# A decoder kernel: two key-partition score items issued together, and batch 1's self-attention groups placed between batch 0's cross-attention groups

## The chip, the cores and the metric

The kernel runs on one core of a Trainium2 chip. The metric is the device time of one execution in microseconds (us), lower is better. Engines: PE is TensorE (PEld its weight loads), DVE is VectorE, ACT is ScalarE, POOL is GpSimd and SP issues most transfers.

## The reference

Two decoder blocks with layer norm after each of six sub-layers, on x of 2 x 512 x 256 and a context of 2 x 1024 x 192, in float32:

```
x = layernorm(x + L0_attn(x))          # 16 heads, causal, 3 score dims and one bias dim, values of 16: "A0"
x = layernorm(x + L0_xattn(x, ctx))    # 16 heads of 16, 1024 keys: "X0"
x = layernorm(x + L0_ffn(x))           # matrices of +1 and -1
x = layernorm(x + L1_attn(x))          # 16 heads of 64: "A1"
x = layernorm(x + L1_xattn(x, ctx))    # 8 heads of 64, 1024 keys: "X1"
x = layernorm(x + L1_ffn(x))           # 8 experts, 2 picked
```

Each attention is a softmax of scores times values, then an output product. The change touches A0 and X0 alone.

## The kernel before

A0 and X0 are worked in **groups** of four heads: (layer, batch, g), 16 groups in all, in the order of the list `PAIRS`. The scores of a group are made twice. In the first pass the queries lie on the partitions, and only the row maximum is kept:

- **S1** (PE, L1576 for X0 on `x_kqF`; L1565 with the mask L1569 for A0 on `a_st`) writes the scores of two heads to one slot of `p_ring`. **M1** (DVE, L1311) reduces them to negated maxima in `halves` or `wide_max`. X0 has 16 such items a group, A0 8.
- **mt** transposes the maxima (PE L1695), and DVE adds them to the queries (`x_q`, `a_q`), so that the second pass subtracts them.

In the second pass the keys lie on the partitions, as the values product wants them:

- **S2** (PE, L1598 for X0, L1590 for A0) writes scores for 128 keys and two heads to a slot of `p_ring`. The contraction is over 32 (17) rows, so that each head uses one of four row groups of TensorE; an item has `pr` 0 or 1 and uses row groups 0, 1 or 2, 3. X0 has 16 items a group, A0 6.
- **E2** (ACT, L1135 and L1139) exponentiates the slot into `prob_a`. **CL** (DVE L1325, X0) clips it; **TM** (POOL L1047, A0) masks it.
- **PV** (PE L1621) multiplies with the values, once for two items. **DN** (ACT L1151) copies the result out, **dt** (PE L1687, DVE L1461 and L1462) and **rb** (PE L1716, DVE L1469) divide by the sums.

`p_ring` has three slots (`RING = 3`), taken in turn by S1 and S2 items as they are issued: an item waits until the one three before it has been read, an S1 item by M1, an S2 item by E2.

Everything else is a **unit**, through the single bank `p_unit`: projections q, k, v, output products **wo** (PE L1531 on `wo_rows`), transposes **xT** (L1675). After wo follow a layer norm (LS, LP, LN: DVE, POOL, DVE) and xT, and the next layer's queries need that.

`paired_stream` writes the order of all engines at build time, as a row of **passes** of one loop. A pass issues at most one S2 item (from the list `second`), at most one S1 item (from the list `first`), the CL or TM of the last one, perhaps one PV, and at most one unit. Both lists follow `PAIRS`. `may_score` lets S1 run ahead of S2 by up to two groups and four items; S2 of a group may start two passes after its mt was read. The engines run their instructions in this order and wait for one another by semaphores, so passes overlap in time.

In the program of before, passes 53 to 216 reach from the first wo of A0 to the last S2 item. Later come the feed-forward layer, A1, X1 and the experts, whose order the change does not touch.

Of the kernel before, what the change touches and what calls it, by code (L numbers as in the profile page):

```python
# [100 lines left out]
PAIRS = [(L, b, g) for L in ("A0", "X0") for b in range(B) for g in range(4)]  # L101
# [43 lines left out]
def paired_stream(sched, chains):  # L145
# [8 lines left out]
    pending, owed, clean, adds, keep = [], [], [], [], []  # L154
# [17 lines left out]
    while f < len(first) or s < len(second) or pending or owed or clean or adds or keep or any(heads):  # L172
# [188 lines left out]
def build_schedule():  # L361
    sched = Schedule()

    def used(n):

        return [("S2", prob_items(PAIRS[n])[-1])] if n >= 0 else []

    def a0_start(b):
# [4 lines left out]
        for g in range(4):  # L373
            out.append(step("DS", "A0", b, g, after=[UD("q", "A0", b)] + used(4 * b + g - HELD)))
# [5 lines left out]
    def x0_keys(b, g):  # L380
        n = 4 * b + g - HELD
        return [unit("k", "X0", b, g, h, after=used(8 + n) if n >= 0 else []) for h in range(2)]

    def x0_queries(b, g):
        n = 4 * b + g - HELD
        return [unit("q", "X0", b, g, after=[turned_x("A0", b)] + (used(8 + n) if n >= 0 else []))]
# [116 lines left out]
def decoder(nc, d, out):  # L503
# [29 lines left out]
    with ctx:  # L533
# [240 lines left out]

        def pair_back(grp, k):
# [78 lines left out]
        def _(sp):  # L854
# [75 lines left out]
            for kind, key in sched.steps:  # L930
# [11 lines left out]
                if L == "A0":  # L942
# [7 lines left out]
                    if grp >= HELD:  # L950
                        wait(sp, "S2", *prob_items(PAIRS[grp - HELD])[-1])
# [46 lines left out]
        def _(pool):  # L998
# [31 lines left out]
            for kind, key in sched.steps:  # L1030
                if kind == "KF":
# [4 lines left out]
                    if 4 * b + g >= HELD:  # L1036
                        wait(pool, "S1", *max_items(PAIRS[8 + 4 * b + g - HELD])[-1])
# [53 lines left out]
        def _(act):  # L1091
# [14 lines left out]
            for kind, key in sched.steps:  # L1106
# [60 lines left out]
                elif kind == "UA":  # L1167
# [18 lines left out]
                    elif u[0] in ("q", "k") and u[1] == "X0":  # L1186
                        _, L, b, g = u[:4]
                        place, part = (4 * b + g) % HELD, u[4] if u[0] == "k" else 2
                        if 4 * b + g >= HELD:
                            wait(act, "S2", *prob_items(PAIRS[8 + 4 * b + g - HELD])[-1])  # L1190
# [41 lines left out]
        def _(dve):  # L1232
# [41 lines left out]
            for kind, key in sched.steps:  # L1274
# [250 lines left out]
        def _(pe):  # L1525
# [8 lines left out]
            for kind, key in sched.steps:  # L1534
# [20 lines left out]
                elif kind == "S1":  # L1555
# [4 lines left out]
                    if L == "A0":  # L1560
                        pe.wait_ge(a0_stacked[G % HELD], 16 * 8 * (G // HELD + 1))
                        w = 128 * (i + 1)
                        for aa in range(2):
                            r = 64 * pr + 32 * aa
                            nc.tensor.matmul(o[:, aa, 0:w], a0_st[r:r + 17, G % HELD, 1, 128 * i:128 * i + 128],  # L1565
                                             a0_st[r:r + 17, G % HELD, 0, 0:w], start=True, stop=False,
# [310 lines left out]
```

## Time and profile before

| | before |
|---|---|
| median of 3 runs | 1334.27 us (1333.01 to 1334.39) |
| the profiled execution | 1329.35 us, its span 1327.6 us |
| PE, DVE, ACT busy, share of the span | 90%, 56%, 42% |
| TensorE's clock as granted, mean over the span | 0.956 |

A profile row gives the start, the duration, the engine, the line, the operation, and what is written and read. A busy share is time in which some instruction of the engine is under way; matmuls are pipelined, so a busy PE may still have room. A float32 matmul of the program is two records in the trace (S2, PV and the units; `x4` for the two heads of one S2 item), an S1 matmul is one. Granted clock 1.00 is TensorE's 2.4 GHz level, 0.50 its 1.2 GHz level. An idle time in brackets names what ended it.

### The profile page before, as it was taken

To read this page: it belongs to the slowest core of one execution; us is meant where nothing else is said; L and a number is where in the kernel's file an instruction comes from. 1 tells how busy PE (TensorE), PEld (TensorE's weight loads), DVE (VectorE), ACT (ScalarE), POOL (GpSimd) and SP (SyncE) were. 2 spreads that over 40 slices of the span, in tenths; PEclk is the share of its full clock that TensorE was granted. 3 is DMA by queue.
4 is the path that set the end of the run, shared out by engine and by line. 5 is a ranking of instruction groups with operands and counts; after the bars stand their busy time and mean duration, and the time that the engine had idled before them with its cause. 6 is when DMAs were issued, how large, how long until landed. Compare 5 with 4: busy or idle time off the path is not lost.

```text
span 1327.6 us, 20645 instructions
## 1 busy us (share of the span) xinstructions
PE 1193.6 (90%) x7754; PEld 754.9 (57%) x7754; DVE 742.4 (56%) x1099; ACT 556.9 (42%) x1070; POOL 89.6 (7%) x127
## 2 busy tenths in 40 slices
PE   5999887899999986889599999999999999998887
PEld 3454444233332234778367777767777777777545
DVE  3346476888898845453256554655455554554322
ACT  1343332555555641221156663655334444453230
POOL 1112211000000003000000000000000000000120
PEclk9898877999999987999799999999999999999989
DMA  5010002000000002000242331223443333120000
GB/s 169 9 49 18 8 1 64 0 1 1 1 1 1 1 1 80 0 0 1 68 119 65 80 80 33 65 64 81 113 120 80 80 81 81 31 50 1 0 16 16
DMA packets 46917, 57.47 MB, mean 43 GB/s; under 512 B 12635, under 2 KB 25446, under 8 KB 46822
## 3 DMA queue, kind: packets, MB, share of 16 engines
q1 hardware_dynamic: 43062, 52.48, 16.3%
q10 hardware_dynamic: 3760, 3.67, 0.9%
q8 instruction: 66, 1.08, 0.3%
q14 instruction: 29, 0.24, 0.1%
HBM read 15.23 MB, written 3.15 MB: 14 GB/s over the span
## 4 chain that ended last, share of the span: by engine, by line
PE 79%; DVE 9%; issue 6%; ACT 3%; POOL 1%; DMA 1%; SPq 1%; POOLq 0%; ACTq 0%; DVEq 0%
PE p_unit L1531 21%; PE p_ring L1531 11%; PE p_ring L1632 9%; PE p_out L1655 8%; PE p_ring L1551 8%; PE p_ring L1598 7%; PE p_out L1621 6%; PE p_unit L1716 2%; PE p_ring L1576 2%; PE p_unit L1675 1%; DVE probT_b L1341 1%; PE p_ring L1590 1%; DVE stats L1244 1%; POOL m_z L1064 1%; PE p_ring L1569 1%
## 5 line engine op out<-in xcount | busy, mean ns | idle before, releaser
L1153 ACT ACTIVATE probT_b<-p_ring 128x512 f32<-128x512 f32 x144 | 84.5, 598 | 260.4 <-PE p_ring L1632 260.0
L1311 DVE TENSOR_REDUCE halves<-p_ring 128x2 f32<-128x1024 f32 x128 | 155.6, 1218 | 40.9 <-PE p_ring L1576 40.7
L1341 DVE COPY probT_b<-p_ring 128x512 f32<-128x512 f32 x112 | 77.4, 691 | 174.0 <-PE p_ring L1632 174.0
L1135 ACT ACTIVATE prob_a<-p_ring 128x1024 f32<-128x1024 f32 x128 | 130.7, 1023 | 93.8 <-PE p_ring L1598 93.8
L1293 DVE TENSOR_REDUCE nmax<-p_ring 128x2 f32<-128x1024 f32 (+1 forms) x128 | 155.9, 1218 | 23.5 <-PE p_ring L1551 23.5
L1121 ACT ACTIVATE prob_b<-p_ring,nmax 128x512 f32<-128x512 f32 (+1 forms) x192 | 158.7, 835 | 2.6 <-DVE nmax L1293 2.3
L1551 PE MATMUL p_ring<-stacks 128*128 128x512 f32 x512 | 150.8, 417 | 4.5 <-ACT prob_b L1121 4.5
L1632 PE MATMUL p_ring<-ident,prob_b 128*128 128x128 f32 x1024 | 134.6, 274 | 0.0
L1632 PEld LDWEIGHTS p_ring<-ident,prob_b 128*128 128x128 f32 x1024 | 115.8, 141 | 27.7 <-issue 25.8
L1598 PE MATMUL p_ring<-x_q,x_kq 32*128 32x512 f32 x512 | 126.5, 656 | 0.0
L1551 PEld LDWEIGHTS p_ring<-stacks 128*128 128x128 f32 x512 | 87.0, 190 | 17.0 <-ACT prob_b L1121 5.1
L1325 DVE TENSOR_SCALAR prob_a<-prob_a 128x1024 f32<-128x1024 f32 x128 | 89.5, 700 | 8.6 <-ACT prob_a L1135 8.6
L1311 DVE TENSOR_REDUCE wide_max<-p_ring 128x2 f32<-128x256 f32 (+3 forms) x64 | 52.5, 823 | 66.4 <-PE p_ring L1569 66.3
L1576 PE MATMUL p_ring<-x_kqF 32*128 32x512 f32 x256 | 66.6, 518 | 16.8 <-ACT prob_a L1135 15.9
L1598 PEld LDWEIGHTS p_ring<-x_q,x_kq 32*128 32x128 f32 x512 | 38.3, 188 | 68.7 <-issue 48.5
L1621 PE MATMUL p_out<-prob_a,x_v 128*32 128x512 f32 x512 | 69.9, 618 | 2.7 <-issue 1.8
L1655 PE MATMUL p_out<-probT_b,a_v 128*64 128x128 f32 x1024 | 70.0, 279 | 0.0
L1655 PE MATMUL p_out<-probT_b,x_v 128*64 128x128 f32 x1024 | 69.6, 279 | 0.0
L1655 PEld LDWEIGHTS p_out<-probT_b,a_v 128*64 128x64 f32 x1024 | 54.6, 136 | 23.4 <-issue 17.5
L1655 PEld LDWEIGHTS p_out<-probT_b,x_v 128*64 128x64 f32 x1024 | 54.6, 136 | 21.9 <-issue 11.3
L1531 PE MATMUL p_unit<-ctxT,x_wk 128*128 128x512 f32 x128 | 66.1, 641 | 0.4
L1487 DVE TENSOR_TENSOR splitL_b<-p_unit,splitH_b 128x512 fp32r<-128x512 f32 x44 | 30.4, 691 | 60.3 <-ACT splitH_b L1198 54.2
(201 smaller groups left out, 1658.6 us busy)
## 6 DMA issues: line engine op xcount, KB each, us to landing
stacks<-splitH_b SPq DMA_DIRECT2D x144, 128.0 KB, 2.4
stacks<-splitL_b SPq DMA_DIRECT2D x144, 128.0 KB, 2.4
a_st<-a_image SPq DMA_DIRECT2D x64, 32.0 KB, 1.8
ctx_raw<-in_ctx ACTq DMA_DIRECT2D x1, 1536.0 KB, 15.5
x<-in_x ACTq DMA_DIRECT2D x2, 512.0 KB, 5.2
k_words<-in_L_ffn_k SPq DMA_DIRECT2D x1, 1024.0 KB, 6.7
a_wq<-in_L_attn_Wq SPq DMA_DIRECT2D x1, 1024.0 KB, 6.2
a_wo<-in_L_attn_Wpost SPq DMA_DIRECT2D x1, 1024.0 KB, 9.3
```

What stands on the lines that cost most here:

```text
L1121: ins = nc.scalar.activation(prob_b[:, n % NP_SLOTS, a * 512:a * 512 + w_all], p_scores[:, n % 2, a * 512:a * 512 + w_all], ACT.Exp, bias= ...
L1135: nc.scalar.activation(prob_place(key), slot_of("S2", key), ACT.Exp, accum_out=x0_sums[:, m:m + 1]).then_inc(done["E2"], 1)
L1293: nc.vector.tensor_reduce(nmax[:, n % 4, 0:heads], src, AX.X, ALU.max, negate=True).then_inc(done["M"], 1)
L1311: nc.vector.tensor_reduce(to, src, AX.X, ALU.max, negate=True).then_inc(done["M1"], 1)
L1341: keep_turned(dve, key, lambda o, i: nc.vector.tensor_copy(o, i)).then_inc(done["VD"], 1)
L1531: ins = nc.tensor.matmul(o, a, m, start=(n == 0), stop=(n == len(pairs) - 1))
L1551: ins = nc.tensor.matmul(p_scores[:, n % 2, 512 * a:512 * a + 512], st[:, q_at:q_at + 128], st[:, k_at:k_at + 512], start=(part == 0), sto ...
L1576: ins = nc.tensor.matmul(o[:, aa, :], x0_kqF[r:r + 32, place, 2, 128 * i:128 * i + 128], x0_kqF[r:r + 32, place, hf, :], start=True, stop= ...
L1598: ins = nc.tensor.matmul(o[:, aa, :], x0_kq[r:r + 32, place, j // 4, 128 * (j % 4):128 * (j % 4) + 128], x0_q2[r:r + 32, G % 2, :], start= ...
L1621: ins = nc.tensor.matmul(p_out[32 * a:32 * a + 32, lo:T], v, prob_place((*key, a // 2))[:, a % 2, at:at + T - lo], start=(c == 0), stop=end)
L1632: ins = nc.tensor.transpose(p_turn[:, half, 128 * j:128 * j + 128], prob_b[:, n % NP_SLOTS, 128 * bl:128 * bl + 128], ident[:, :])
L1655: ins = nc.tensor.matmul(p_out[rows * a:rows * a + rows, 128 * i:128 * i + 128], values(L, b, h, j), probT[:, n % places, 4 * in_tile + j ...
```

## The change

Two edits. First, `PAIRS` no longer finishes A0 of batch 1 before X0 of batch 0: after A0 (1,0) and (1,1) come X0 (0,0), A0 (1,2), X0 (0,1), A0 (1,3), and then the other X0 groups. Second, S2 items are issued two at a time, `pr` 0 and 1, every second pass, so that four heads on four row groups stand together; their E2s still go one to a pass. The rest adapts the addressing: places in `a0_st`, `x0_kq` and `x0_kqF` come from batch and g in place of the position in `PAIRS`, and waits name the group by layer.

```diff
-PAIRS = [(L, b, g) for L in ("A0", "X0") for b in range(B) for g in range(4)]
+PAIRS = ([("A0", 0, g) for g in range(4)] + [("A0", 1, 0), ("A0", 1, 1), ("X0", 0, 0), ("A0", 1, 2), ("X0", 0, 1)]
+         + [("A0", 1, 3), ("X0", 0, 2), ("X0", 0, 3)] + [("X0", 1, g) for g in range(4)])
...
         fresh = []
-        if s < len(second) and age("UD", "mt", *second[s][:3]) >= 2:
-            it = second[s]
-            s += 1
-            sched.add("S2", *it)
+        if not scored and s < len(second) and age("UD", "mt", *second[s][:3]) >= 2:
+            for it in second[s:s + 2]:
+                sched.add("S2", *it)
+                scored.append(it)
+            s += 2
+        if scored:
+            it = scored.pop(0)
             sched.add("E2", *it)
             fresh.append(it)
...
+        def place_of_heads(grp):
+
+            return (4 * grp[1] + grp[2]) % HELD
...
                     else:
-                        place = (G - 8) % HELD
+                        place = place_of_heads((L, b, g))
```

On PE, in the middle of an X0 group with no unit near, the program of before has this (L1598 is S2, L1576 is S1, L1621 is PV):

```order
L1598 MATMUL p_ring<-x_q,x_kq 128x512 x2
L1576 MATMUL p_ring<-x_kqF 128x512 x2
L1598 MATMUL p_ring<-x_q,x_kq 128x512 x2
L1576 MATMUL p_ring<-x_kqF 128x512 x2
L1621 MATMUL p_out<-prob_a,x_v 32x512 x4
```

The changed program has this, where the lines have moved by 13 (L1611 is S2, L1589 S1, L1634 PV):

```order
L1611 MATMUL p_ring<-x_q,x_kq 128x512 x4
L1589 MATMUL p_ring<-x_kqF 128x512 x2
L1634 MATMUL p_out<-prob_a,x_v 32x512 x4
L1589 MATMUL p_ring<-x_kqF 128x512 x2
```

Two S2 items of two heads have become one run of four heads, the first S1 item stands behind all four, and the second S1 item behind PV.

On PE, where S1 of X0 (0,0) is issued, the program of before has this (L1590 is S2 of A0, L1687 and L1716 are dt and rb):

```order
L1590 MATMUL p_ring<-a_q,a_st 128x512 x2
L1576 MATMUL p_ring<-x_kqF 128x512 x2
L1590 MATMUL p_ring<-a_q,a_st 128x384 x2
L1576 MATMUL p_ring<-x_kqF 128x512 x2
L1687 MATMUL p_unit<-ident,raw 128x128 x4
L1590 MATMUL p_ring<-a_q,a_st 128x384 x2
L1576 MATMUL p_ring<-x_kqF 128x512 x2
```

The changed program has this there, up to the first v unit of batch 1's X0 (L1544 on `x_wv`):

```order
L1589 MATMUL p_ring<-x_kqF 128x512 x4
L1700 MATMUL p_unit<-ident,raw 128x128 x4
L1589 MATMUL p_ring<-x_kqF 128x512 x2
L1729 MATMUL p_unit<-ident,rwide_a 128x128 x4
L1589 MATMUL p_ring<-x_kqF 128x512 x24
L1544 MATMUL p_unit<-x_wv,ctxT 128x256 x4
```

No S2 item is left between the S1 items: fifteen of the sixteen stand in these rows, with dt and rb alone between them.

On PE, the two wo units of A0 batch 1 stand like this in the program of before:

```order
L1531 MATMUL p_unit<-wo_rows,outT_a 128x256 x8
L1576 MATMUL p_ring<-x_kqF 128x512 x2
L1695 MATMUL p_unit<-ident,wide_max 128x128 x4
L1576 MATMUL p_ring<-x_kqF 128x512 x2
L1531 MATMUL p_unit<-wo_rows,outT_a 128x256 x8
```

In the changed program they come much later, in X0 (0,2):

```order
L1611 MATMUL p_ring<-x_q,x_kq 128x512 x4
L1589 MATMUL p_ring<-x_kqF 128x512 x2
L1544 MATMUL p_unit<-wo_rows,outT_a 128x256 x8
L1589 MATMUL p_ring<-x_kqF 128x512 x2
L1544 MATMUL p_unit<-wo_rows,outT_a 128x256 x8
L1611 MATMUL p_ring<-x_q,x_kq 128x512 x4
```

Before, only S1 work stood around them; now S2 work does too.

## Rows read from the trace of the kernel before

**Rows 1.** The page: busy time by engine; granted clock in 40 slices.

```profile
PE 1193.6 (90%) x7754; PEld 754.9 (57%) x7754; DVE 742.4 (56%) x1099; ACT 556.9 (42%) x1070; POOL 89.6 (7%) x127
...
PEclk9898877999999987999799999999999999999989
```

**Rows 2.** The page: shares of the chain that ended last.

```profile
PE 79%; DVE 9%; issue 6%; ACT 3%; POOL 1%; DMA 1%; SPq 1%; POOLq 0%; ACTq 0%; DVEq 0%
```

**Rows 3.** Windows: length, then busy time (and instructions) of PE, PEld, DVE, ACT, POOL; clock.

```profile
124.00:215.00 91.00, 79.35 (x460) 44.18 (x460) 52.82 (x80) 24.00 (x33) 16.02 (x29) 0.85 0.03 7
...
324.00:456.00 132.00, 122.79 (x697) 39.72 (x696) 116.31 (x147) 74.03 (x136) 5.55 (x9) 1.00 0.00 1
```

**Rows 4.** Timeline of DVE in X0, no unit near.

```profile
341.57 1.21 DVE L1311 TENSOR_REDUCE halves<-p_ring 128x2 f32<-128x1024 f32 x1
342.70 0.68 DVE L1325 TENSOR_SCALAR prob_a<-prob_a 128x1024 f32<-128x1024 f32 x1
343.30 1.22 DVE L1311 TENSOR_REDUCE halves<-p_ring 128x2 f32<-128x1024 f32 x1
...
350.52 1.22 DVE L1311 TENSOR_REDUCE halves<-p_ring 128x2 f32<-128x1024 f32 x1 [0.21 <-PE p_ring L1576]
```

**Rows 5.** Timeline of PE and ACT in the same stretch.

```profile
345.53 0.70 PE L1598 MATMUL p_ring<-x_q,x_kq 32*128 32x512 f32 x2
345.55 0.50 PE L1576 MATMUL p_ring<-x_kqF 32*128 32x512 f32 x2
...
346.71 1.02 ACT L1135 ACTIVATE prob_a<-p_ring 128x1024 f32<-128x1024 f32 x1 [1.58 <-PE p_ring L1598]
...
347.88 0.50 PE L1576 MATMUL p_ring<-x_kqF 32*128 32x512 f32 x2 [0.45 <-ACT prob_a L1135]
348.31 1.07 PE L1621 MATMUL p_out<-prob_a,x_v 128*32 128x512 f32 x8
```

**Rows 6.** Timeline of PE in X0 where units k and q stand.

```profile
326.51 1.98 PE L1531 MATMUL p_unit<-ctxT,x_wk 128*128 128x512 f32 x4
328.42 0.70 PE L1598 MATMUL p_ring<-x_q,x_kq 32*128 32x512 f32 x2
...
329.48 1.98 PE L1531 MATMUL p_unit<-xT,x_wq 128*128 128x512 f32 x4
```

**Rows 7.** Timeline of PE after the last S1 item.

```profile
471.13 1.14 PE L1598 MATMUL p_ring<-x_q,x_kq 32*128 32x512 f32 x8
472.20 1.06 PE L1621 MATMUL p_out<-prob_a,x_v 128*32 128x512 f32 x8
473.20 1.13 PE L1598 MATMUL p_ring<-x_q,x_kq 32*128 32x512 f32 x6
```

**Rows 8.** Timeline of DVE (S1 without CL) and of ACT (S2 without S1).

```profile
171.12 3.47 DVE L1311 TENSOR_REDUCE halves<-p_ring 128x2 f32<-128x1024 f32 x3
...
473.32 1.02 ACT L1135 ACTIVATE prob_a<-p_ring 128x1024 f32<-128x1024 f32 x1
...
474.38 1.02 ACT L1135 ACTIVATE prob_a<-p_ring 128x1024 f32<-128x1024 f32 x1
```

**Rows 9.** Timeline of ACT in A0.

```profile
118.59 1.02 ACT L1139 ACTIVATE prob_a<-p_ring 128x1024 f32<-128x1024 f32 x1 [3.46 <-PE p_ring L1590]
...
124.71 0.81 ACT L1139 ACTIVATE prob_a<-p_ring 128x768 f32<-128x768 f32 x1 [1.17 <-PE p_ring L1590]
```

**Rows 10.** Timeline of PE: units v, wo and xT of batch 1.

```profile
184.80 3.78 PE L1531 MATMUL p_unit<-x_wv,ctxT 128*128 128x256 f32 x8
...
189.99 1.99 PE L1531 MATMUL p_unit<-x_wv,ctxT 128*128 128x256 f32 x8
...
198.85 5.38 PE L1531 MATMUL p_unit<-wo_rows,outT_a 128*128 128x256 f32 x16 [0.67 <-DVE outT_a L1469]
...
207.52 3.72 PE L1531 MATMUL p_unit<-wo_rows,outT_a 128*128 128x256 f32 x16 [0.63 <-DVE x_q L1455]
```

**Rows 11.** Window at the low clock, columns as in rows 3.

```profile
219.80:233.50 13.70, 11.91 (x44) 4.33 (x44) 8.84 (x11) 4.76 (x9) 2.35 (x1) 0.50 0.06 11
```

More of the change, by code:

```diff
@@ L153, in paired_stream @@
     heads = [list(c) for c in chains]
-    pending, owed, clean, adds, keep = [], [], [], [], []
+    pending, owed, clean, adds, keep, scored = [], [], [], [], [], []
     f = s = n = 0
@@ L170, in ready @@
         return item[0] <= n and all(a in sched.at for a in item[2])
-    while f < len(first) or s < len(second) or pending or owed or clean or adds or keep or any(heads):
+    while f < len(first) or s < len(second) or pending or owed or clean or adds or keep or scored or any(heads):
         while pending:
@@ L373, in a0_start @@
         for g in range(4):
-            out.append(step("DS", "A0", b, g, after=[UD("q", "A0", b)] + used(4 * b + g - HELD)))
+            out.append(step("DS", "A0", b, g, after=[UD("q", "A0", b)] + used("A0", 4 * b + g - HELD)))
         return out
@@ L381, in x0_keys @@
         n = 4 * b + g - HELD
-        return [unit("k", "X0", b, g, h, after=used(8 + n) if n >= 0 else []) for h in range(2)]
+        return [unit("k", "X0", b, g, h, after=used("X0", n)) for h in range(2)]
     def x0_queries(b, g):
         n = 4 * b + g - HELD
-        return [unit("q", "X0", b, g, after=[turned_x("A0", b)] + (used(8 + n) if n >= 0 else []))]
+        return [unit("q", "X0", b, g, after=[turned_x("A0", b)] + used("X0", n))]
     last_one = prob_items(PAIRS[-1])[-1]
@@ L950, in _ @@
                     if grp >= HELD:
-                        wait(sp, "S2", *prob_items(PAIRS[grp - HELD])[-1])
+                        wait(sp, "S2", *prob_items(("A0", (grp - HELD) // 4, (grp - HELD) % 4))[-1])
                     for which in range(2):
@@ L1036, in _ @@
                     if 4 * b + g >= HELD:
-                        wait(pool, "S1", *max_items(PAIRS[8 + 4 * b + g - HELD])[-1])
+                        wait(pool, "S1", *max_items(x0_back(b, g))[-1])
                     nc.gpsimd.tensor_copy(x0_kqF[:, place, part, :], x0_kq[:, place, part, :]).then_inc(done["KF"], 1)
@@ L1189, in _ @@
                         if 4 * b + g >= HELD:
-                            wait(act, "S2", *prob_items(PAIRS[8 + 4 * b + g - HELD])[-1])
+                            wait(act, "S2", *prob_items(x0_back(b, g))[-1])
                         if u[0] == "q":
@@ L1564, in _ @@
                             r = 64 * pr + 32 * aa
-                            nc.tensor.matmul(o[:, aa, 0:w], a0_st[r:r + 17, G % HELD, 1, 128 * i:128 * i + 128],
-                                             a0_st[r:r + 17, G % HELD, 0, 0:w], start=True, stop=False,
+                            nc.tensor.matmul(o[:, aa, 0:w], a0_st[r:r + 17, place_of_heads(key[:3]), 1, 128 * i:128 * i + 128],
+                                             a0_st[r:r + 17, place_of_heads(key[:3]), 0, 0:w], start=True, stop=False,
                                              tile_position=(r, 0))
@@ L1594, in _ @@
                     else:
-                        place = (G - 8) % HELD
+                        place = place_of_heads((L, b, g))
                         for aa in range(2):
```

15 lines of the change are left out of this document (9 added, 6 removed).

## The prediction

> **What bounds the kernel now.** I read the page first. PE is busy 90% of the span and DVE 56% [rows 1], and the chain that ended last lies on PE for 79% [rows 2]. So a change to the order counts where it lets PE wait less or do less. The clock slices [rows 1] show 8, 8, 7, 7 in slices 4 to 7 (33.2 us each, so 100 to 232 us), which hold the end of A0 and the start of X0, and 9 in the seven slices behind them.
>
> Then I read the windows. From the first wo of A0 to the first S2 of X0 (124 to 215 us) PE is busy for 79.35 of 91 us at clock 0.85, and DVE for 52.82, so DVE stands idle for 38 us [rows 3]. In the X0 groups of batch 1 (324 to 456 us) PE is busy for 122.79 of 132 us, and DVE for 116.31, 88% [rows 3]. Here two engines are near their limits together.
>
> The timeline says which of them sets the pace. With no unit near, M1 follows CL by 0.60 us and CL follows M1 by 1.13 us, so DVE alone wants 1.73 us a pass. From 341.57 to 350.52 us lie five passes, 1.79 us each [rows 4]. DVE sets this pace. PE there runs S2 and S1 at once: S1 starts 0.02 us after S2, on other row groups [rows 5]. Where units stand, PE sets the pace: unit k takes 1.91 us up to the next S2, and S2 with its S1 hidden beneath takes 1.06 us up to the next unit [rows 6].
>
> **Edit one, four heads back to back.** I cost two passes of X0 on PE.
> - Before: two S2 with hidden S1 (2 x 1.06) [rows 6] and one PV (1.00, from 472.20 to 473.20 us) [rows 7] make 3.12 us.
> - After: four heads together take 1.07 us (eight records, from 471.13 to 472.20 us; four records took 1.06) [rows 6]. But all four row groups are now taken, so the first S1 stands behind S2, and the second, behind PV, has no S2 beside it either. Each costs 0.43 us (from 347.88 to 348.31 us) [rows 5]. With PV that is 2.93 us.
>
> So a pair saves 0.19 us of PE, not 1.06. It saves nothing at all where DVE sets the pace. There another loop comes near. S2, S2, S1, S1 share three slots, so the first S1 of a pair of passes takes the slot of the S1 just before it. It must wait for that M1 to end: M1 1.22, a release, S1 0.50 [rows 5]. With 0.07 us for two releases that is 1.79 us from M1 to M1 against 1.73, so two passes take 3.52 to 3.6 us, as now. ACT's loop is shorter: E2 starts 1.18 us after S2 (345.53 to 346.71) [rows 5], two E2 take 2 x 1.06 [rows 8], 3.3 us in all. For A0 I see the same exchange with smaller pieces. About a dozen pairs lie beside k and q in X0, which saves 2 us; the dt and rb units lose about as much, because their PE work now queues behind an S1 that is out in the open. I take 0 for this edit, with -9 (some 45 full pairs at 0.19) and +8 (the same 45, were the two releases 0.18 us slower together) as bounds.
>
> The Trainium skill has a rule that speaks for the edit: the page TensorE: Matmul & The Clock Gate, section Part 3: Packing small matmuls, gives four row tiles of 512 columns a speedup of 3.07 over running them one by one. Rows 7 agree that four heads cost what two cost. By that rule alone the sum would lose one S2 for every pair.
>
> **Edit two, A0 and X0 alternate.** It removes and adds no work; it changes which items meet in a pass. I counted the passes of the two programs by what they issue, S1 / S2, from the first wo of A0 to the last S2: 164 before, 185 now. S1 of X0 (0,0) now stands alone (the second place of the order shown above), and the lead that `may_score` allows is counted in groups, so that an A0 group of 6 items holds back an X0 group of 16. The prices are from the rows, with bounds where no row has the case.
> - X0 / X0: 109 to 89, at 1.79 [rows 4]: -35.8.
> - A0 / A0: 13 to 1, at 1.53 (118.59 to 124.71 us, four passes) [rows 9]: -18.4.
> - X0 / none: 12 to 27, at 1.16 (3.47 us for three) [rows 8]: +17.4.
> - none / X0: 19 to 29, at 1.06 (473.32 to 474.38 us) [rows 8]: +10.6.
> - A0 / none: 4 to 6, at 1.53: +3.1.
> - X0 / A0: 7 to 12. Before, at DVE's 1.16. Now the pair's loop of M1, release and S1 has no CL to hide in: half of (1.79 + 1.16), 1.48. 12 x 1.48 - 7 x 1.16: +9.6. (At 1.16 it would be +5.8.)
> - A0 / X0: 0 to 10. No row shows it. The bounds are ACT's 1.06 and the X0 pace of 1.79; I take half of ACT's loop of 3.3, 1.65: +16.5 (+10.6 to +17.9).
> - none / A0: 0 to 7. Bounds 0.81 (E2 alone) [rows 9] and 1.53; I take 1.1: +7.7.
> - none / none: 0 to 4, units alone: 0, as they are counted below.
>
> The sum is +10.7 us. One list alone is cheap for a pass, but 1.16 and 1.06 make 2.22 us for what one full pass does in 1.79.
>
> **The units that move.** The order of edit two puts batch 1's two wo beside S2 work, and the four v beside S1 of A0. PE still needs 3.72 us for each wo and 1.99 for each v [rows 10], and the ring gives DVE and ACT at most three slots to live on meanwhile, so they are not hidden. What can be gained is clock: the first v took 3.78 and the first wo 5.38 us [rows 10], 1.79 and 1.66 us more than their fellows. I take -3 for that and for a layer norm with more work beside it. The bounds are 0, if the new stretch of S1 alone (PE at work 0.43 of 1.16 us) takes the clock down ahead of the v units again, and -15, over a third of DVE's 38 idle us [rows 3] refilled. Transfers play no part: the a_st loads wait for A0's S2 items, which come no later than their use needs, and later stages load early.
>
> **Sum.** 0 + 10.7 - 3, so +8 us. The profiled execution took 1329.35 us, 1.75 of it outside its span of 1327.6; with the change it would take 1337.4. The median of the runs lies 4.9 us above the profiled execution, so I predict 1342 us. A difference within 0.2% (2.7 us) could hardly be told from none.
>
> **Rivals.**
> - *The alternation fills the idle time* (faster). DVE's 38 idle us from 124 to 215 us [rows 3] and A0's light items under X0's S2 are what speaks for it: the refill is then -15, the two unseen kinds of pass cost their lower bounds (-6 -4 -2 against the sum), and the pairs save 7 of the 9 us: 10.7 - 12 - 15 - 7, about -23 at the very best; with half of each, 10.7 - 6 - 10 - 5, -10: 1324 us. It decides when refill and pairs together pay over 11 us. Against it: 21 more passes. Chance 0.22.
> - *The pairs pay in full* (faster), as by the rule of the page above. 64 pairs at 1.06 us are 68 us of PE, but DVE's busy share of 88% in X0 [rows 3] leaves 12% of the 260 us or so from 215 us on, 31 us, and the alternation takes 8 back: 1311 us. Against it: S1 is hidden now. Chance 0.03.
> - *The clock falls* (slower still). In two full passes PE would have 2.93 us of work in 3.55 us, against 3.12 in 3.58 now, and the new stretches of S1 alone have 0.43 us in 1.16 [rows 5, 8]. At 0.50 DVE was busy for 8.84 of 13.7 us, 65% against 88% [rows 11, 3], so a stretch there costs a quarter of its length. With 40 us more at 0.50: +10, 1352 us. For it: slices 6 and 7 stand at 7 already, behind passes of this thin kind at 171 us [rows 1, 8]. Against: it held in slices 8 to 14, where full passes ran. Chance 0.18.
> - *Nothing to measure*: the singles cost less and the refill pays for them. 1334 us. Chance 0.12.
>
> The Trainium skill's page TensorE: Matmul & The Clock Gate, section Why this matters for your kernels, warns of PE idle gaps between bursts; by that the third rival would be likelier than I put it, and [rows 1] agree in that the dips lie where PE is least busy.
>
> **Numbers.** The forecast itself (1335 to 1349) has 0.45. Slower by over 0.2%: 0.45 and 0.18, 0.63. Same: 0.12. Faster: 0.22 and 0.03, 0.25. The range goes from 1322, which takes in half-successful filling, to 1355 for the clock.
>
> **What would show it.** In the profile after: eight S2 records in 1.14 us with S1 after them; full X0 passes still at 1.75 to 1.8 us; S1 of X0 (0,0) as sixteen reductions 1.16 us apart with ACT idle for 25 us or more; the first S2 of X0 (0,3) 5 to 12 us later than now; the last X0 group ending about 8 us later; the rest of the span unchanged. I am wrong on edit one if an X0 group of batch 1 takes over 1 us less or over 2 us more than now, and on edit two if S2 of X0 (0,3) starts earlier than now. What would make the forecast fail most easily is the clock, which my prices hold at 1.00.

## The result, and the profile after

| | before | after |
|---|---|---|
| median | 1333.64 us (1327.12 to 1334.39, 4 runs) | 1364.03 us (1360.38 to 1368.97, 4 runs) |
| ratio | | 1.0243, 95% interval 1.0204 to 1.0282 |
| span of the profiled execution | 1327.6 us | 1362.2 us |
| mean granted clock | 0.956 | 0.927 |

The change costs 30 us. The forecast of 1342 us had the direction, and its range ended at 1355, 9 us below the median. The ratios below leave out two executions of other kernels, one of run 5 (1695.4 us at a clock of 0.64, and its trace is of this one) and one of run 13 (1355.4 us).

The kernel before stood beside the runs in 58 more executions, at mean clocks of 0.938 to 0.954 and 1327.0 to 1342.4 us. Its profiled one had 0.956, more than any of them, so what is read below from one trace against another holds somewhat more clock than the medians do.

The page of the changed kernel: busy times, granted clock in slices of 34.1 us, and the shares of the chain that ended last.

```profile
PE 1204.9 (88%) x7754; PEld 762.5 (56%) x7754; DVE 744.4 (55%) x1099; ACT 552.3 (41%) x1070; POOL 90.0 (7%) x127
...
PEclk7996778687999998799899999999999999999998
...
PE 72%; DVE 17%; issue 5%; ACT 3%; DMA 1%; POOL 1%; SPq 1%; POOLq 0%; DVEq 0%; ACTq 0%
```

Against [rows 1, 2], PE's busy time is only 11 us longer, and the chain has moved from PE (79% to 72%) to DVE (9% to 17%). The clock slices 4 to 10 (102 to 341 us) read 6, 7, 7, 8, 6, 8, 7, where slices 4 to 10 of before read 8, 8, 7, 7, 9, 9, 9.

Where the end of the interleaving stands is shown by the first E2 of X0 (0,3), the first E2 of X0 (1,0) and the last E2 of X0. Timeline of ACT after:

```profile
363.72 1.02 ACT L1148 ACTIVATE prob_a<-p_ring 128x1024 f32<-128x1024 f32 x1 [0.47 <-PE p_ring L1611]
...
399.62 1.02 ACT L1148 ACTIVATE prob_a<-p_ring 128x1024 f32<-128x1024 f32 x1 [0.47 <-PE p_ring L1611]
...
516.97 1.02 ACT L1148 ACTIVATE prob_a<-p_ring 128x1024 f32<-128x1024 f32 x1
```

These three stood at 325.63, 360.98 and 481.10 us before. So the changed kernel is 38.1 us late at X0 (0,3), 38.6 at X0 (1,0), and 35.9 at the end of X0. The whole loss is made by 364 us.

Windows of the kernel before (length, then busy time of PE, PEld, DVE, ACT, POOL, granted clock): up to the first E2 of X0 (0,3), from pass 53 on, passes 37 to 53, and from pass 53 to the first reduction of X0.

```profile
0.00:325.70 325.70, 281.40 (x1640) 131.49 (x1644) 202.88 (x291) 127.39 (x210) 43.73 (x87) 0.92 0.12 33
125.20:325.70 200.50, 177.52 (x1048) 76.91 (x1048) 144.88 (x195) 82.69 (x141) 23.15 (x36) 0.90 0.05 13
100.90:125.20 24.30, 22.45 (x188) 11.13 (x184) 16.64 (x26) 11.40 (x15) 5.83 (x12) 0.84 0.10 24
125.20:169.40 44.20, 38.75 (x250) 20.21 (x246) 22.24 (x40) 14.67 (x21) 11.80 (x19) 0.90 0.03 7
```

The same windows of the changed kernel, and last its stretch of X0 (0,0) reductions alone:

```profile
0.00:364.00 364.00, 304.55 (x1648) 140.85 (x1652) 203.99 (x291) 125.63 (x211) 45.45 (x88) 0.81 0.10 29
131.50:364.00 232.50, 196.89 (x1052) 84.91 (x1052) 145.50 (x195) 81.40 (x141) 24.70 (x37) 0.79 0.04 11
102.00:131.50 29.50, 27.16 (x188) 13.15 (x190) 16.82 (x25) 11.03 (x15) 5.84 (x13) 0.67 0.07 19
131.50:169.40 37.90, 29.92 (x134) 15.14 (x134) 8.07 (x19) 9.03 (x13) 9.13 (x13) 0.76 0.03 7
169.40:187.90 18.50, 12.80 (x57) 5.92 (x58) 18.41 (x18) 0.87 (x2) 0.62 (x1) 0.62 0.00 1
```

A window's clock of c means that 2 x (1 - c) of its length ran at 0.50 (1.2 GHz) and the rest at 1.00 (2.4 GHz). From pass 53 to X0 (0,3) the kernel before has 40 us at 0.50 in 200.5, the changed one 98 in 232.5. Passes 37 to 53 hold the same work in both, but for the pairs: 24.3 us at 0.84 and 29.5 at 0.67 (they come back in run 8). And in the window up to the first reduction of X0, which stands at 169.4 us in both kernels, DVE worked 22.24 us before and 8.07 after.

### The profile page after: what moved, and what is told of

The parts are those of the page before. It is cut to its first block, busy times and chain, and to the rows that moved or that the text cites. A ratio compares the mean times of both kernels' runs of the same rounds, so it can differ in the third digit from the quotient of the medians.

```text
span 1362.2 us, 20645 instructions
## 1 busy us (share of the span) xinstructions
PE 1204.9 (88%) x7754; PEld 762.5 (56%) x7754; DVE 744.4 (55%) x1099; ACT 552.3 (41%) x1070; POOL 90.0 (7%) x127
## 4 chain that ended last, share of the span: by engine, by line
PE 72%; DVE 17%; issue 5%; ACT 3%; DMA 1%; POOL 1%; SPq 1%; POOLq 0%; DVEq 0%; ACTq 0%
PE p_unit L1544 20%; PE p_ring L1544 11%; PE p_ring L1645 8%; PE p_out L1668 8%; PE p_ring L1564 7%; DVE halves L1324 6%; PE p_out L1634 4%; PE p_ring L1611 4%; DVE prob_a L1338 2%; PE p_unit L1729 2%; PE p_unit L1688 1%; PE p_ring L1578 1%; PE p_ring L1589 1%; DVE probT_b L1354 1%; DVE stats L1257 1%
## 5 line engine op out<-in xcount | busy, mean ns | idle before, releaser
L1611 PE MATMUL p_ring<-x_q,x_kq 32*128 32x512 f32 x512 | 85.4, 689 | 12.2 <-ACT prob_a L1148 12.0
L1589 PE MATMUL p_ring<-x_kqF 32*128 32x512 f32 x256 | 73.5, 596 | 11.2 <-DVE halves L1324 10.0
L1589 PEld LDWEIGHTS p_ring<-x_kqF 32*128 32x128 f32 x256 | 25.4, 204 | 87.9 <-DVE halves L1324 40.9
L1634 PE MATMUL p_out<-prob_a,x_v 128*32 128x512 f32 x512 | 71.6, 632 | 0.5 <-issue 0.5
L1544 PE MATMUL p_unit<-ctxT,x_wk 128*128 128x512 f32 x128 | 65.3, 633 | 1.5 <-ACT x_kq L1208 1.3
```

The lines of the kernel that those rows point to most:

```text
L1544: ins = nc.tensor.matmul(o, a, m, start=(n == 0), stop=(n == len(pairs) - 1))
L1589: ins = nc.tensor.matmul(o[:, aa, :], x0_kqF[r:r + 32, place, 2, 128 * i:128 * i + 128], x0_kqF[r:r + 32, place, hf, :], start=True, stop= ...
L1611: ins = nc.tensor.matmul(o[:, aa, :], x0_kq[r:r + 32, place, j // 4, 128 * (j % 4):128 * (j % 4) + 128], x0_q2[r:r + 32, G % 2, :], start= ...
L1634: ins = nc.tensor.matmul(p_out[32 * a:32 * a + 32, lo:T], v, prob_place((*key, a // 2))[:, a % 2, at:at + T - lo], start=(c == 0), stop=end)
```

## The experiments

All times are beside runs of the kernel before on the same chip, whose medians were 1334.3 to 1335.8 us. In short:

| kernel | median, us | ratio, 95% interval |
|---|---|---|
| pairs alone (1) | 1352.49 | 1.0143 (1.0094 to 1.0192) |
| order alone (2) | 1358.44 | 1.0177 (1.0137 to 1.0218) |
| after, S1 three times (3) | 1377.31 | 1.0333 (1.0277 to 1.0390) |
| before, S1 three times (4) | 1338.82 | 1.0038 (1.0011 to 1.0065) |
| old order, pairs of X0 (5) | 1334.24 | 0.9995 (0.9968 to 1.0021) |
| old order, pairs of A0 (6) | 1352.15 | 1.0131 (1.0080 to 1.0182) |
| new order, pairs of X0 (7) | 1352.08 | 1.0127 (1.0061 to 1.0192) |
| order alone, S1 twice (8) | 1365.85 | 1.0220 (1.0175 to 1.0265) |
| weakened order, no pairs (9) | 1341.93 | 1.0050 (1.0031 to 1.0069) |
| as 6, S1 ahead of the pair (10) | 1347.80 | 1.0118 (1.0066 to 1.0169) |
| as 9, pairs of X0 (11) | 1338.39 | 1.0021 (0.9998 to 1.0043) |
| old order, pairs of A0 batch 1 (12) | 1343.37 | 1.0071 (1.0040 to 1.0103) |
| old order, pairs of A0 batch 0 (13) | 1348.35 | 1.0085 (1.0049 to 1.0120) |

**1. The pairs alone.**

```diff
-PAIRS = ([("A0", 0, g) for g in range(4)] + [("A0", 1, 0), ("A0", 1, 1), ("X0", 0, 0), ("A0", 1, 2), ("X0", 0, 1)]
-         + [("A0", 1, 3), ("X0", 0, 2), ("X0", 0, 3)] + [("X0", 1, g) for g in range(4)])
+PAIRS = [(L, b, g) for L in ("A0", "X0") for b in range(B) for g in range(4)]
```

> The changed kernel with the old order of head groups: edit one (two passes' S2 matmuls issued together) alone. Theory A (the time is mostly TensorE's clock: the trace of the changed kernel has 170.6 us at a granted clock of 0.50 before its time 600, against 88.6 before the change): the pairs leave the order alone, so 1334 to 1342, with low-clock time as in the kernel before. Theory B (more passes and passes that hold one kind of work cost it): 1334, since the number of passes is unchanged. Theory C (the pairs cost it, by the 6 us that the all-A0 stage to step 53 lost and 0.5 us in each of the eight X0 groups): 1342 to 1346. My own forecast had edit one at 0.

It measured +18, more than any theory gave. An edit that I had put at 0 costs over half of the loss by itself. Its trace puts nearly all of it ahead of X0's second passes: pass 78, which lies behind A0's last reduction (pass 69), is 28.8 us late in that execution, the first E2 of X0 (0,3) 31 us, and the last E2 of X0 28 us.

**2. The order alone.**

```diff
-            for it in second[s:s + 2]:
-                sched.add("S2", *it)
-                scored.append(it)
-            s += 2
+            it = second[s]
+            s += 1
+            sched.add("S2", *it)
```

> The changed kernel with one S2 issued per pass, as before: edit two (the order of head groups) alone. Theory A (clock): 1352 to 1362, with some 50 us or more of added time at a granted clock of 0.50 in the stretch from 125 to 360. Theory B (the ledger of passes, which my forecast priced at +10.7 less 3): 1342, with the clock as before. Theory C (pairs): what the whole change cost less what the pairs alone do, 1355.

It measured +24, inside theory A's range of times. The two parts sum to 42 us and the whole is 30, so they overlap. Windows of it, as above: up to the first E2 of X0 (0,3), from pass 53, passes 37 to 53.

```profile
0.00:351.00 351.00, 296.56 (x1640) 137.19 (x1644) 202.87 (x291) 127.19 (x210) 43.66 (x87) 0.84 0.11 30
127.60:351.00 223.40, 191.81 (x1048) 82.67 (x1048) 144.45 (x195) 82.86 (x141) 23.18 (x36) 0.83 0.04 11
98.60:127.60 29.00, 27.90 (x188) 13.40 (x192) 16.87 (x25) 11.38 (x15) 5.80 (x12) 0.62 0.07 20
```

The first window is 25.3 us longer than before, with the same number of PE instructions (1640), and has 112 us at 0.50 against 52. But in the order that `paired_stream` writes, this kernel and the one before are the same up to pass 53. So the second window is what the order can account for: 22.9 us longer, with 76 us at 0.50 against 40. These 36 us are fewer than the 50 that theory A wanted, and the other 24 of the 60 us at 0.50 fell into passes that the order does not touch.

**3 and 4. Keeping TensorE busy**, in the changed kernel and in the one before.

```diff
+    beside = {sched.when[(kind, key)] for kind, key in sched.steps if kind == "E2" and key[0] == "X0"}
+
+    def times(key):
+        return 1 if sched.when[("S1", key)] in beside else 3
...
+                        for again in range(times(key)):
                             for aa in range(2):
```

> The changed kernel with every S1 matmul of X0 done three times over, with the same result, in the passes that have no E2 of X0 (the passes in which VectorE's reduction sets the pace and TensorE streams for less than half of it). Nothing is left out, six matmul instructions stand where two stood. Theory A: TensorE is busier where it idled, the 0.50 stretches between 150 and 335 shrink by half or more, and 10 to 20 us of the 30 come back, to 1344 to 1354. Theories B and C: the repeats are work added to passes that VectorE bounds, so nothing comes back, 1364, or up to 10 us more where they run at half clock and become the bound.

> The kernel before with the same repeats of S1 of X0 in passes without an E2 of X0. Theory A: the 20 us or so at 0.50 between 175 and 234 of the kernel before shrink, and with them 3 to 8 us, 1326 to 1331. Theories B and C: no gain, 1334 to 1340.

Nothing came back: 13 us more than the changed kernel, and 4 more than the one before. Three S1 at 0.43 us would want 1.29 us in a pass of 1.13, but in the stretch of X0 (0,0) reductions the repeats were no bound: twelve reductions took 13.66 us, as in the changed kernel (13.67). Windows of that stretch in the kernel of 3:

```profile
174.76:179.30 4.54, 3.53 (x24) 1.63 (x20) 4.54 (x6) 0.00 (x0) 0.00 (x0) 1.00 0.01 4
179.30:188.40 9.10, 8.97 (x40) 6.45 (x41) 9.10 (x9) 0.00 (x0) 0.00 (x0) 0.50 0.00 0
```

The clock fell to 0.50 in the middle of the repeats and stayed there while PE was busy for 8.97 of 9.10 us. So more work for PE did not hold it up here. Where the 13 us are lost stays open; the profiled execution loses 9 of them by X0 (0,3), behind that stretch. Run 8 repeats less.

**5 and 6. Which pairs cost.** Both keep the old order.

```diff
-            for it in second[s:s + 2]:
+            together = 2 if second[s][0] == "X0" else 1
+            for it in second[s:s + together]:
                 sched.add("S2", *it)
                 scored.append(it)
-            s += 2
+            s += together
```

(and "A0" for "X0" in the other)

> Old order, S2 issued in pairs for X0's items only, singly for A0's. In the trace of the pairs-alone kernel the E2 of A0's step 53 comes 14.6 us later than before and the groups of X0 stand at the distances of before. Theory D: a pair takes two of the three score slots, so that the S1 of its pass waits for VectorE's reduction of the pass before, and that costs only in A0, where the reductions set the pace; TensorE sets it in X0. Then this kernel is at 1331 to 1338, no change. Theory C, all pairs cost by their count (24 of A0's to 64 of X0's): 1346 or so.

> Old order, pairs for A0's items only. Theory D: the whole +18 of the pairs-alone kernel, 1348 to 1356, with a part of it (8 or so) in stretches where the S1 of a pair's pass waits at the full clock, and the rest in time at a granted clock of 0.50 between 98 and 160. Theory C: 1339.

64 of 88 pairs are X0's and cost nothing; the 24 of A0 cost all 18 us. Theory D foretold these times. It says that a pair takes two of the three slots, so that an S1 waits for the reduction of the pass before. In passes of A0 without a unit such waits can be read. The kernel before, PE and then DVE:

```profile
95.60 0.44 PE L1565 MATMUL p_ring<-a_st 17*128 17x384 f32 x2
...
96.19 0.44 PE L1590 MATMUL p_ring<-a_q,a_st 17*128 17x384 f32 x2
96.99 0.44 PE L1565 MATMUL p_ring<-a_st 17*128 17x384 f32 x2 [0.36 <-ACT prob_a L1139]
```

```profile
96.30 0.96 DVE L1311 TENSOR_REDUCE wide_max<-p_ring 128x2 f32<-128x768 f32 x1 [0.92 <-PE p_ring L1569]
97.68 0.96 DVE L1311 TENSOR_REDUCE wide_max<-p_ring 128x2 f32<-128x768 f32 x1 [0.42 <-PE p_ring L1569]
```

And the kernel with pairs of A0, passes 34 and 35, PE and then DVE:

```profile
95.19 0.44 PE L1578 MATMUL p_ring<-a_st 17*128 17x384 f32 x2
...
96.11 0.55 PE L1603 MATMUL p_ring<-a_q,a_st 17*128 17x384 f32 x4 [0.26 <-ACT prob_a L1152]
96.90 0.44 PE L1578 MATMUL p_ring<-a_st 17*128 17x384 f32 x2 [0.24 <-DVE wide_max L1324]
```

```profile
95.89 0.96 DVE L1324 TENSOR_REDUCE wide_max<-p_ring 128x2 f32<-128x768 f32 x1 [0.80 <-PE p_ring L1582]
97.60 0.96 DVE L1324 TENSOR_REDUCE wide_max<-p_ring 128x2 f32<-128x768 f32 x1 [0.75 <-PE p_ring L1582]
```

With pairs, S1 at 96.90 us waits for DVE: its slot is that of the reduction at 95.89, which has only just ended at 96.85. The next reduction starts at 97.60, and DVE stood idle 0.75 us, where it stood 0.42 in the kernel before. There the S1 at 96.99 waits for ACT, and the reduction of the pass before (96.30) is still running, so they overlap.

Passes 25 to 33, one A0 group with its units, are at a clock of 1.00 in both, and show what a group pays. Windows of the kernel before (with passes 17 to 78, and 78 to X0 (0,3), for what follows):

```profile
54.70:182.30 127.60, 116.16 (x794) 60.41 (x792) 70.95 (x104) 53.29 (x73) 29.09 (x55) 0.89 0.07 20
182.30:325.70 143.40, 127.27 (x723) 51.34 (x724) 111.43 (x144) 62.35 (x114) 8.44 (x11) 0.92 0.05 15
75.20:94.70 19.50, 18.86 (x132) 11.75 (x128) 7.90 (x13) 8.53 (x14) 2.91 (x6) 1.00 0.15 43
```

and of the kernel with pairs of A0:

```profile
54.40:206.70 152.30, 138.56 (x796) 69.16 (x800) 72.26 (x105) 53.12 (x73) 29.82 (x56) 0.72 0.06 17
206.70:345.40 138.70, 122.34 (x720) 48.76 (x721) 111.25 (x144) 61.58 (x113) 7.77 (x10) 0.95 0.06 16
73.90:94.40 20.50, 19.48 (x136) 11.99 (x132) 8.10 (x13) 8.55 (x14) 3.06 (x6) 1.00 0.14 41
```

19.5 us become 20.5, so the pairs cost 1.0 us a group at the full clock; for eight groups that is 8 us, an estimate. But this isn't the wait of theory D. PE is busy for 19.48 of 20.5 us there and DVE for 8.10, so PE sets the pace, and none of PE's idle time there ends with an S1 or S2 that waited for a slot. What has changed is what PE hides. The kernel before, where units stand:

```profile
77.47 0.50 PE L1590 MATMUL p_ring<-a_q,a_st 17*128 17x512 f32 x2
77.48 0.44 PE L1565 MATMUL p_ring<-a_st 17*128 17x384 f32 x2
...
78.23 1.99 PE L1531 MATMUL p_unit<-x_wv,ctxT 128*128 128x256 f32 x8
```

and the kernel with pairs of A0:

```profile
78.98 0.45 PE L1603 MATMUL p_ring<-a_q,a_st 17*128 17x384 f32 x4
79.27 0.34 PE L1578 MATMUL p_ring<-a_st 17*128 17x384 f32 x2
...
82.15 0.46 PE L1603 MATMUL p_ring<-a_q,a_st 17*128 17x256 f32 x8
82.64 0.50 PE L1578 MATMUL p_ring<-a_st 17*128 17x512 f32 x2
```

Before, S2 starts 0.01 us ahead of S1 and lies wholly beneath S1 and its mask, which take 0.76 us up to the unit. With pairs, S1 starts 0.29 and 0.49 us behind the first of the two S2, and 0.34 us in the third pair of the group (93.52 to 93.86 us): 1.12 us in all. The passes that now have no S2 save nothing, for S1 and mask alone still take 0.75 us up to the unit (76.31 to 77.06 us). That is about the 1.0 us measured.

From pass 17 to 78 the loss is 24.7 us in this execution, and the clock of that stretch fell from 0.89 to 0.72, 57 us more at 0.50. Behind pass 78, where the two programs are the same, it is 4.7 us faster than before, at 0.95 against 0.92.

**7. The new order with pairs of X0 only.** The diff is the first of 5, on the changed kernel.

> The new order with pairs for X0's items only, A0's singly. Theory D: the changed kernel less what the pairs of A0 cost it, which the two parts' sum (+18 and +24 against +30 for both) puts at 6: 1356 to 1360, as the order alone. If pairs of X0 cost something in the interleaved stretch, where A0's S1 stands beside X0's S2: 1360 to 1364.

1352.08: below both expectations. A0's pairs are worth 12 us of the changed kernel, and X0's pairs beside A0's reductions seem to save some 6 against the order alone, but the intervals overlap, and the four executions are two of 1346 us at clocks of 0.939 and 0.941 and two of 1358 and 1360 us at 0.929. So this can be the clock of two executions.

**8. The order alone, S1 doubled in passes without any E2.** As 3, with `beside` over the E2 of both layers and 2 for 3.

> The new order with S2 issued singly, and every S1 matmul of X0 done twice in the passes that have no E2 of any kind (some 29 passes, in which a reduction of 1.13 us sets the pace and S1 takes 0.43 us at the full clock, so that 0.86 still hides). Nothing is left out. Theory A (the rest of the order's +24 over the ledger's +8 is time at 0.50): the low-clock time between 164 and 191 shrinks and the units and passes right behind it run at the full clock, 1348 to 1355. Theory B: 1358, no change, since those passes wait for the reductions at either clock; up to 1362 if two matmuls at half clock (1.7 us) outlast the reduction.

Theory A's cure fails: 1365.85, and the clock is no higher. Windows of this kernel: passes 37 to 53, and the 16 reductions of X0 (0,0) alone.

```profile
99.60:131.40 31.80, 31.44 (x188) 14.36 (x192) 16.95 (x24) 11.31 (x15) 5.83 (x12) 0.50 0.08 18
166.00:185.30 19.30, 16.96 (x86) 8.53 (x84) 18.44 (x19) 0.60 (x1) 0.62 (x1) 0.62 0.00 1
```

In the second, PE was busy for 16.96 of 19.3 us, against 12.99 of 18.7 in the order alone, and the clock is 0.62 in both. The first lies ahead of every doubled instruction, and holds the same work as in the order alone, but took 31.8 us at 0.50 against 29.0 at 0.62. More kernels give it with the same work: 24.3 us at 0.84 before, and the new order with pairs of X0, and last run 11 below:

```profile
99.00:124.90 25.90, 24.57 (x189) 11.88 (x192) 16.64 (x25) 11.42 (x15) 5.82 (x12) 0.76 0.09 22
...
100.20:132.05 31.85, 31.49 (x188) 14.42 (x192) 16.98 (x25) 11.36 (x15) 5.80 (x12) 0.50 0.07 18
```

These lie on a line: 24.3, 25.9, 29.0 and 31.8 us with 7.8, 12.4, 22.0 and 31.8 us at 0.50, which is (31.8 - 24.3) / (31.8 - 7.8) = 0.31 us lost for each us at 0.50. Run 4 (25.2 us at 0.76) and run 9 (28.7 at 0.62) lie near it.

In the order that `paired_stream` writes, all seven kernels are the same up to pass 53. So what differs between these seven is not the change of order. The two with the old order have the least time at 0.50, but it is one execution of each, and they can't say whether that is more than chance. The clock has a price there; what sets it stays open.

**9 to 11. A weaker order, and the ring or the queue.**

```diff
-PAIRS = ([("A0", 0, g) for g in range(4)] + [("A0", 1, 0), ("A0", 1, 1), ("X0", 0, 0), ("A0", 1, 2), ("X0", 0, 1)]
-         + [("A0", 1, 3), ("X0", 0, 2), ("X0", 0, 3)] + [("X0", 1, g) for g in range(4)])
+PAIRS = ([("A0", 0, g) for g in range(4)] + [("A0", 1, 0), ("A0", 1, 1), ("A0", 1, 2), ("X0", 0, 0)]
+         + [("A0", 1, 3), ("X0", 0, 1), ("X0", 0, 2), ("X0", 0, 3)] + [("X0", 1, g) for g in range(4)])
```

> S2 issued singly, and the new order weakened: the key order is A0 of batch 0 (4 groups), A0 of batch 1 groups 0 to 2, X0(0,0), A0(1,3), X0(0,1) and the rest. The passes that hold an S1 or an E2 are 219 up to pass 249, against 211 before and 230 in the order alone. Theory B (the number of passes prices it; the order alone has 19 more and costs 24): 8/19 of 24, 1344. Theory E (the order's cost is that S1 of X0(0,0), which must wait for batch 0's layer norm, stands ahead of A0(1,2)'s S1, so that no reduction runs for about 31 us and 16 of X0 then run alone): A0(1,2)'s S1 fill that time again as they do before, and little is left, 1334 to 1338. Theory A (clock): anywhere between, with 0.2 to 0.34 us for each us more at a granted clock of 0.50 than before's 55 up to the first E2 of X0(0,3).

> The weakened order of the one-crossing kernel with pairs for X0's items only. Pairs of X0 were worth nothing in the old order and 6 us (1352 against 1358, intervals touching) in the new one. If those 6 us are real and come from passes in which X0's S2 stands beside A0's reductions: 3 us below the one-crossing kernel. If they were chance of the clock: the same as it within 3.

+7 us, where the count of passes gives +10 and theory E up to +4. It lies between the two and tells neither out. Most of the order's cost is gone when A0 (1,2) may be reduced while batch 0's layer norm runs; the passes are fewer too, so this doesn't show which of the two did it. With pairs of X0 the median is another 3.5 us lower, as expected if run 7's 6 us were real, but the intervals overlap.

Run 10, in the loop that writes the schedule:

```diff
+        begin = not scored and s < len(second) and age("UD", "mt", *second[s][:3]) >= 2
+        early = begin and second[s][0] == "A0"
+        if early:
+            reduce_one()
...
+        if not early:
+            reduce_one()
```

(`reduce_one` is the block that adds S1 and M1.)

> Old order, pairs for A0's items only, and in a pass that begins a pair the S1 and its reduction ahead of the two S2 instead of behind them. Theory D1 (the score ring: with three slots, two taken by a pair, every S1 of one of the two passes takes the slot of the reduction just before it, and cannot overlap it): the slots come round in the same cycle, nothing is gained, 1348 to 1356. Theory D2 (TensorE's queue: the S1 stands behind two S2 that wait for ScalarE): the S1 is free of them and 8 or more us come back, 1334 to 1344.

1347.80 is at the lower edge of D1's 1348 to 1356 and 4 us outside D2's. Passes 25 to 33 take 20.8 us in its trace, against 20.5 with S1 behind the pair and 19.5 without pairs. So in that stretch nothing is gained, and an S1 that stands behind waiting S2 isn't what costs. This doesn't speak for the ring alone: with S1 first, the pair stands in the open behind the mask (from 94.56 to 95.00 us in its trace), where it would cost as much. No run kept the pairs and gave the ring a fourth slot, so the two aren't told apart by a run; the rows above are what speaks for the work in the open.

**12 and 13. Half of the pairs of A0.**

```diff
-            together = 2 if second[s][0] == "A0" else 1
+            together = 2 if second[s][:2] == ("A0", 1) else 1
```

(and 0 for 1 in the other)

> Old order, pairs only for the A0 items of batch 1 (four of the eight A0 groups); those of batch 0, before step 48, go singly. Theory D with the ring's price alone, 1.0 us a group (passes 25 to 33, at the full clock in both kernels, take 20.5 us with pairs and 19.5 without): 1338. If the clock's share belongs to the pairs too, half of the 18: 1343. If it is chance that fell in passes 37 to 53, which hold singles here: 1338 to 1340.

> Old order, pairs only for the A0 items of batch 0. Ring alone: 1338. With the clock's share bound to the pairs of passes 37 to 48 (wholly at 0.50 in both traces with pairs in them and old order): 1343 to 1348, and then the two halves' surpluses over before should sum to the 17 to 18 of all A0 pairs.

By their ratios they cost 9.5 and 11.4 us, 21 in all, against 17.5 for both halves at once. Each costs more than the 4 us of four groups at 1.0 (both intervals lie above it), so the rest comes with the pairs too. The traces, one execution of each, have it at the pairs: with pairs in batch 1 only, passes 37 to 53 take 24.5 us as before and passes 53 to 64 take 38.7 against 31.8; with pairs in batch 0 only, it is 32.6 and 33.9. That alone would be weak, since run 11 has 31.8 us in passes 37 to 53 without a pair of A0.

## Why the prediction fell short

**Edit one, put at 0 (bounds -9 and +8), measured +18.** This is the step that failed, and in it the sentence on A0. For X0 the working held. The changed kernel in X0, PE and then DVE:

```profile
381.80 1.07 PE L1634 MATMUL p_out<-prob_a,x_v 128*32 128x512 f32 x8
382.80 0.50 PE L1589 MATMUL p_ring<-x_kqF 32*128 32x512 f32 x2
383.52 1.24 PE L1611 MATMUL p_ring<-x_q,x_kq 32*128 32x512 f32 x8 [0.22 <-ACT prob_a L1148]
384.93 0.50 PE L1589 MATMUL p_ring<-x_kqF 32*128 32x512 f32 x2 [0.17 <-DVE halves L1324]
```

```profile
381.92 1.22 DVE L1324 TENSOR_REDUCE halves<-p_ring 128x2 f32<-128x1024 f32 x1
...
383.65 1.22 DVE L1324 TENSOR_REDUCE halves<-p_ring 128x2 f32<-128x1024 f32 x1
...
385.47 1.23 DVE L1324 TENSOR_REDUCE halves<-p_ring 128x2 f32<-128x1024 f32 x1
```

The eight records of S2 take 1.24 us (I said 1.14, and 1.07 in the sum), S1 starts 1.41 us after them, it waits for the M1 before it (the loop that I described, "M1 1.22, a release, S1 0.50"), and two passes take 3.55 us (381.92 to 385.47), in the forecast 3.52 to 3.6. Pairs of X0 alone measured 0.9995. What failed is the one sentence on A0, "the same exchange with smaller pieces". It is not the same exchange. In X0 an S2 with its S1 beneath takes 1.06 us and S1 alone 0.43, so a pair takes two long pieces together and puts two short ones in the open. In A0 the longer piece is S1 with its mask, 0.76 us, and S2 was hidden beneath it; a pair puts S2's 0.29 to 0.49 us in the open and saves nothing. Where no unit stands, the waits for the ring come on top (0.26 us for ACT and 0.24 for DVE in passes 34 and 35). X0 has a CL of 0.6 us behind each M1, under which the next S1 is written; in A0 DVE has nothing between two M1. Together that is 1.0 us a group at the full clock where it was measured. My bound of +8 was worked out for X0's pairs, and that it equals eight groups of A0 is luck. The other 10 us I had no term for: they go with time at 0.50, 57 us more from pass 17 to 78. At 0.31 those would be 18, and 18 + 8 overstates the 24.7 us there by little.

**Edit two, put at +10.7 for the ledger and -3 for units, measured +24.** From pass 53 on, where the order begins to differ, the order alone is 22.9 us longer up to X0 (0,3), with 36 us more at 0.50. At 0.31 that is 11 us and leaves 12, more than the forecast's 7.7 and near the ledger's 10.7 without the gain that I took for the units. This is an estimate: the price is from passes 37 to 53 alone, a clock is given to 0.01, which is up to 2 us of each window at 0.50, and where reductions set the pace the price is nothing, as the next rows show, which would leave more for the ledger. So the ledger's sum is not refuted, and not confirmed to better than a few us. What it lacked is what the forecast said of it, the clock, "which my prices hold at 1.00". The weaker order (8 more passes for +7, where 19 cost 24) costs less for each pass, but within the intervals.

**The units.** I gave -3 for a better clock of v and wo. The pair of wo of batch 1 in the changed kernel:

```profile
314.87 4.90 PE L1544 MATMUL p_unit<-wo_rows,outT_a 128*128 128x256 f32 x16
...
321.34 3.72 PE L1544 MATMUL p_unit<-wo_rows,outT_a 128*128 128x256 f32 x16 [1.15 <-DVE stats L1257]
```

4.90 and 3.72 us against 5.38 and 3.72 [rows 10]: 0.5 us gained. Against it stands what I did not cost, and what no run here prices by itself. `first` is a queue. S1 of X0 (0,0) must wait for the layer norm of batch 0, as it did before, and now stands ahead of the S1 of A0 (1,2). Timeline of DVE and then of ACT after:

```profile
169.42 3.57 DVE L1324 TENSOR_REDUCE halves<-p_ring 128x2 f32<-128x1024 f32 x3 [13.48 <-PE p_ring L1589]
...
175.46 13.67 DVE L1324 TENSOR_REDUCE halves<-p_ring 128x2 f32<-128x1024 f32 x12
```

```profile
190.33 0.60 ACT L1224 ACTIVATE x_v<-p_unit 128x512 f32<-128x512 f32 x1 [19.50 <-PE p_unit L1544]
...
198.20 1.02 ACT L1148 ACTIVATE prob_a<-p_ring 128x1024 f32<-128x1024 f32 x1 [0.47 <-PE p_ring L1611]
```

The reductions of X0 start at 169.42 us after 13.48 idle us, no earlier than before (169.38), and A0's 16 reductions that used to be done by then are still to come. So the shape that I foretold is there, sixteen reductions 1.13 us apart (I said 1.16). ACT is then idle for 19.50 us in one piece (I said 25 or more), and the stretch is at a clock of 0.62 without loss: the last twelve reductions, at 0.50 throughout, come as fast as those of [rows 8].

**The rivals.** "The clock falls" (0.18) happened, and larger: I allowed 40 us more at 0.50 for +10, and there were 86 us more up to X0 (0,3) (138 against 52). Its price of a quarter is near the 0.31 measured. What it had as the reason, PE with less to do, isn't shown: in run 8 passes 37 to 53 stood at 0.50 with PE busy for 31.44 of 31.80 us. That the clock "held in slices 8 to 14, where full passes ran" stayed true behind 364 us only. The alternation didn't fill idle time: DVE stood idle for more of 131 to 169 us than before. In its price is a slip: half of 15 and of 7 are 7.5 and 3.5, not 10 and 5, so its middle case should have read -6 and 1328 us. "Pairs pay in full" (0.03) was rightly small.

**How much is the clock.** The 58 executions of the kernel before give a price with not an instruction changed. A straight line through their times and their time at 0.50 (from the mean clocks) has 0.29 us for each us at 0.50, 95% interval 0.23 to 0.35. By the mean clocks of all their executions, the pairs alone, the order alone and the pairs of A0 spend 40 to 42 us more at 0.50 than the kernel before beside them, the two halves of A0's pairs 17 and 23, and the changed kernel about 52. At 0.29 that is 12 us for each of the first three, 5 and 7 for the halves, and 15 of the changed kernel's 30. Of the mean times it leaves some 6 us for the pairs of A0 (8 by the count of groups), 4 for each half (4 by the same count), and 13 for the order. These are estimates.

**What stays open** is why the clock falls more with A0's pairs and with the new order. That it does is shown by the mean clocks: 0.926 to 0.931 in the four executions of the changed kernel, 0.931 to 0.934 in those of the order alone, 0.929 to 0.932 with pairs of A0, and 0.938 to 0.954 in the 58 of the kernel before. The three attempts to hold it up failed. Nothing tried beats the kernel before; pairs of X0 alone equal it.

The Trainium skill, page TensorE: Matmul & The Clock Gate, section A second HAM failure mode: psum-queue depth-cycling, tells of a kernel whose clock oscillates because TensorE idles briefly between groups of matmuls as it cycles through PSUM. In the kernel with pairs of A0 the clock does fall at 98.8 us, just behind an S1 that waits for a slot (96.90 us, above), but run 11 spent passes 37 to 53 wholly at 0.50 without a pair of A0, and no run here separates such short waits from the rest. The same page says in Part 1 that the same kernel, as it starts, leaves the low clock at another point from run to run. The executions here differ later in the kernel too: passes 37 to 53, the same in order and work in runs 2 and 8, stood at 0.62 in one and at 0.50 in the other.

## What to carry to other kernels

Before matmuls are brought together, write down for every layer which of them lies beneath which, and how long each is, and not only for the layer whose rows were looked at: a pair that is free where S2 is the long piece (X0) costs where S2 was hidden beneath S1 and its mask (A0). When two streams share a ring, write down too for each item whose slot it takes. Before interleaving two lists, ask what the head of each queue waits for; work that is ready must not stand behind work that isn't. And don't read the clock's share of a change from one trace against another: here the same kernel spread over 15 us with its clock, and about half of a loss of 2.4% goes with TensorE's clock.

## What the runs showed of the hardware

- The same 188 matmuls of passes 37 to 53 took 24.3 to 31.8 us in seven kernels whose order is the same up to there, by the share that was granted 0.50. Each us at 0.50 lost 0.31 us, in passes where PE was busy for 22.45 of 24.3 us. A v unit alone on PE lost more: 3.78 us at 0.50 against 1.99 at 1.00 [rows 10].
- One unchanged kernel ran from 1327.0 to 1342.4 us in 58 executions, and most of that goes with its mean granted clock (0.29 us for each us at 0.50).
- Where DVE sets the pace, half the clock cost nothing: reductions of X0 came 1.14 us apart from 175.46 to 189.13 us, where the clock was 0.50.
- Repeating PE's matmuls in such a stretch did not raise the clock: doubled, PE was busy for 16.96 of 19.3 us at 0.62, against 12.99 of 18.7 at 0.62; threefold, the clock fell to 0.50 among the repeats and stayed there with PE busy for 8.97 of 9.10 us.
- Two S2 items on four row groups kept the next S1 waiting for 0.29 to 0.49 us in A0, where S1 started 0.01 us after a single S2.
